# A median by bisection beside a convolution network: masks summed by TensorE in place of counting chunks on VectorE

## What is computed

```python
q_in = jnp.quantile(x.reshape(B, C, -1), 0.5, axis=-1)
x = x + jax.nn.relu(-q_in)[:, :, None, None]
y = upfirdn2d(x, lpf, up=2, padding=padding, gain=4.0)
y = jnp.maximum(y, 0.0)
y = upfirdn2d(y, lpf, down=2, padding=0, gain=1.0)
# second layer, shortened
spec = jnp.fft.rfft2(x, norm='ortho')
gate = sigmoid(w2 @ gelu(w1 @ abs(spec)))
xf = x + jnp.fft.irfft2(spec * gate, norm='ortho')
out = attention(q(xf), keys_and_values(xf)) @ proj_w + proj_b + x
```

## Time and profile before

| | |
|---|---|
| median of 3 runs | 12846.2 us (12845.59 to 12851.24) |
| the profiled execution | 12841.47 us, span 12840.0 us |
| PE busy | 10730.5 us (84%) |
| PEld busy | 5483.5 us (43%) |
| DVE busy | 9433.9 us (73%) |
| ACT busy | 7283.6 us (57%) |
| POOL busy | 2610.8 us (20%) |
| mean granted TensorE clock | 0.904 of 2.4 GHz |
| GpSimd's addition into Z (L1216) | 64 times, 4.5 us each |

### The profile page before, as it was taken

The page is one execution under the profiler, slowest core; times in us unless marked ns, Lnnn a source line. Parts: engine busy times, 40 slices in busy tenths (PEclk is TensorE's granted clock), DMA queues, the critical chain, the costliest instruction groups (busy, mean ns, idle before and its releaser), DMA issues. The chain is left out here.

```text
span 12840.0 us, 193091 instructions
## 1 busy us (share of the span) xinstructions
PE 10730.5 (84%) x70049; PEld 5483.5 (43%) x70049; DVE 9433.9 (73%) x16044; ACT 7283.6 (57%) x12109; POOL 2610.8 (20%) x4040
## 2 busy tenths in 40 slices
PE   1797888978879798897988889788897887979889
PEld 1543535334353443534435354353534435344353
DVE  7867667776777767768777686767777677776776
ACT  4656455564646646466464565646566464664646
POOL 1211202112131221302212021121211213122130
PEclk9898898988989899898998989889898898989989
DMA  1021120211202022120211202112021221202212
GB/s 45 18 43 42 39 61 18 50 35 43 57 26 55 21 49 52 28 67 7 54 47 34 66 13 46 43 40 60 18 53 31 45 56 27 53 21 49 52 28 66
DMA packets 169035, 532.27 MB, mean 41 GB/s; under 512 B 64008, under 2 KB 86536, under 8 KB 153168
## 3 DMA queue, kind: packets, MB, share of 16 engines
q1 hardware_dynamic: 168016, 519.00, 17.2%
HBM read 230.38 MB, written 67.11 MB: 23 GB/s over the span
## 5 line engine op out<-in xcount | busy, mean ns | idle before, releaser
L949 DVE TENSOR_REDUCE R<-ps 128x2 f32<-128x640 f32 x4096 | 3195.4, 818 | 941.5 <-PE ps L687 930.6
L1157 ACT ACTIVATE R<-ps 128x512 f32<-128x512 f32 x5120 | 2823.2, 594 | 671.5 <-PE ps L708 645.3
L236 ACT ACTIVATE R<-R,st 128x1475 bf16<-128x1475 f32 x1326 | 2022.9, 1526 | 862.5 <-DVE st L312 687.6
L300 DVE TENSOR_SCALAR_CACHE_REDUCE R<-R,st 128x1255 bf16<-128x1255 f32 x1326 | 2012.0, 1517 | 21.3
L687 PE MATMUL ps<-KST,R 96*128 96x320 bf16 x8192 | 1888.4, 314 | 60.7 <-DVE R L949 50.5
L733 PE MATMUL ps<-R 128*32 128x512 f32 x12288 | 1648.8, 609 | 38.0 <-DVE Wk L903 32.9
L708 PE MATMUL ps<-R,KST 104*128 104x512 bf16 x4096 | 1583.7, 389 | 21.4 <-ACT R L1157 20.6
L687 PEld LDWEIGHTS ps<-KST,R 96*128 96x128 bf16 x8192 | 764.8, 100 | 828.6 <-DVE R L949 313.0
L1245 POOL CAST R<-Wk 128x512 bf16<-128x512 f32 x256 | 283.8, 1109 | 2980.4 <-DVE Wk L903 2980.4
L201 PE MATMUL ps<-st,cst 128*128 128x3 f32 x884 | 176.0, 269 | 697.7 <-DVE R L300 464.4
L480 PE MATMUL ps<-R,cst 128*64 128x512 f32 x2048 | 648.5, 715 | 109.0 <-DVE R L818 109.0
(11 more groups left out here) (208 smaller groups left out, 19968.1 us busy)
## 6 DMA issues: line engine op xcount, KB each, us to landing
R<-R SPq DMA_DIRECT2D x3072, 64.0 KB, 2.4
R<-xh_in SPq DMA_DIRECT2D x136, 512.0 KB, 4.5
...
```

The source lines that it names most:

```text
L236: e.activation(junka[:, 0:o2 - o1], xc[:, o1:o2], ACT.Sign, bias=mid, scale=-1.0, accum_out=cnt[:, NP + i:NP + i + 1]).then_inc(md_ca, 1)
L300: e.tensor_scalar(junk[:, 0:o1 - o0], xc[:, o0:o1], mid, None, ALU.is_le, ALU.add, accum_out=cnt[:, i:i + 1]).then_inc(md_cv, 1)
L949: e.tensor_reduce(MX[(4 * u + s4) % 2][:, blk_, h0:h0 + 2], ps[:, 2 + 2 * bq:4 + 2 * bq, 0:320], axis=AX.X, op=ALU.max).then_inc(mx, 1)
L1157: e.activation(PB[:, t % 2, w, :], ps[:, w % 2, :], ACT.Exp).then_inc(ex, 1)
```

## The change

In each of the 26 steps VectorE writes two masks of 2560 columns (2.0 where the value is at most the midpoint, bf16), ScalarE takes signs of two chunks of 1536, TensorE adds the masks up over partition halves in 32 products of 160 columns with a 64-column weight `pairb`, into PSUM bank 7, and VectorE sums the 160 columns there. A step keeps three parts; the third holds the products and that sum. The bracket is plus and minus the largest magnitude: four reductions in four parts, the first midpoint 0, and all bracket widths by one product with a constant row `halves`. The recount is dropped; the masks of the minimum pass (now bf16, BIG a power of two) are added up by TensorE too. That pass goes to the parts right behind the search. ScalarE runs the first part of a pass ahead of the Relu instead of behind it. GpSimd adds the edge rows into Z four rows at a time, in four passes (for the last 16 rows all four in pass 36), and the transfers and the FFT groups wait for those counts. SyncE's last load of TAP2 waits for the end of the median. The mask buffers use the free end of R1. The diff, without the closing chain's renumbered waits; of the median's generators only the new lines and their surroundings are shown ("..." also stands where old lines went):

```diff
-NP = 3
-CUTS = [HALF * i // NP for i in range(NP + 1)]
-MIDS = [a + int(0.46 * (b - a)) for a, b in zip(CUTS, CUTS[1:])]
-SIGNED = sum(b - m for m, b in zip(MIDS, CUTS[1:]))
-FEWER = float(RANK - SIGNED)
+MASKS = ((0, 2560), (4096, 6656))
+SIGNS = ((2560, 4096), (6656, 8192))
+SUM = 160
+SIGNED = sum(b - a for a, b in SIGNS)
+FEWER = 2.0 * (RANK - SIGNED)
 P = C // 2
 MID = 5
...
@@ -85,9 +86,10 @@
...
-        junk = R5[:, 0:1024].bitcast(BF16)
-        junka = R5[:, 1024:2048].bitcast(BF16)
-        tmp = R5[:, :]
+        MK = [R5[:, 0:1280].bitcast(BF16), R1[:, 8320:9600].bitcast(BF16)]
+        junka = R5[:, 1280:2048].bitcast(BF16)
+        MF = [R5[:, 512 * i:512 * i + 512].bitcast(BF16) for i in range(2)]
+        TF = [R5[:, 1024:2048], R1[:, 8320:9344]]
...
@@ -186,29 +188,46 @@
                 self.reader = (md_g, self.asked)
 
         def pe_median(e, b7):
...
+            def sums(mask, width, first, last):
+                n = mask.shape[1] // (2 * width)
+                for q in range(n):
+                    for j in range(2):
+                        o = width * (2 * q + j)
+                        op = e.matmul(ps[64 * j:64 * j + 64, 7, 336:336 + width], lhsT=pairb[:, :], rhs=mask[:, o:o + width],
+                                      start=first and q == 0, stop=last and q == n - 1)
+                return op
+
+            for _ in range(4):
                 yield
             e.wait_ge(md_v, 1)
             b7.free(e)
...
+            e.matmul(P0(1), lhsT=c("swap"), rhs=pm[:, 0:1], start=True, stop=True).then_inc(md_p, 1)
             b7.ask()
             for k in range(STEPS):
...
+                yield
+                yield
+                e.wait_ge(md_cv, 2 * k + 2)
+                b7.free(e)
+                sums(MK[0], SUM, True, False)
+                sums(MK[1], SUM, False, True).then_inc(md_s, 1)
+                b7.reader = (md_r, k + 1)
+                yield
+                e.wait_ge(md_ca, 2 * k + 2)
+                b7.free(e)
+                e.matmul(P0(3), lhsT=c("pair"), rhs=cnt[:, 0:3], start=True, stop=True).then_inc(md_p, 1)
+                b7.ask()
+            for i in range(9):
+                if i < 8:
+                    e.wait_ge(md_ta, i + 1)
+                    b7.free(e)
+                    sums(MF[i % 2], 128, i == 0, i == 7).then_inc(md_fs, 1)
+                yield
+                if i > 0:
                     yield
...
+            b7.reader = (md_r, STEPS + 1)
             b7.free(e)
...
+            e.matmul(P0(1), lhsT=c("pair"), rhs=cnt[:, 0:1], start=True, stop=True).then_inc(md_p, 1)
             b7.ask()
...
             e.wait_ge(md_row, 1)
             b7.free(e)
             e.transpose(ps[0:1, 7, 384:512], pm[:, 0:1], c("ident")).then_inc(md_p, 1)
@@ -224,27 +243,27 @@
             e.matmul(ps[:, 7, 448:512], lhsT=ones[:, :], rhs=dg, start=True, stop=True).then_inc(md_p, 1)
 
         def act_median(e):
...
+            for _ in range(4):
                 yield
             for k in range(STEPS):
                 mid = mids[:, k % 2:k % 2 + 1]
                 e.wait_ge(md_v, 2 + k)
...
+                for i, (o1, o2) in enumerate(SIGNS):
                     if k or i:
...
+                        e.wait_ge(md_ca, 2 * k + i)
                     e.activation(junka[:, 0:o2 - o1], xc[:, o1:o2], ACT.Sign, bias=mid, scale=-1.0,
...
+                                 accum_out=cnt[:, 1 + i:2 + i]).then_inc(md_ca, 1)
                     yield
...
                 yield
+            for _ in range(17 + 2):
+                yield
 
         def pool_median(e):
...
+            for _ in range(4):
                 yield
             for k in range(STEPS):
                 mid = mids[:, k % 2:k % 2 + 1]
...
+                for i in range(3):
                     yield
                 e.wait_ge(md_g, 2 + k)
                 if k:
@@ -252,13 +271,12 @@
...
             for i in range(9):
                 if i < 8:
...
                     e.wait_ge(md_ta, i + 1)
...
+                    if i > 1:
+                        e.wait_ge(md_mm, i - 1)
+                    e.tensor_tensor(TF[i % 2], MF[i % 2], xc[:, 1024 * i:1024 * i + 1024], ALU.add).then_inc(md_tb, 1)
                 yield
                 if i > 0:
                     yield
@@ -269,73 +287,57 @@
             for k in range(4):
                 if halves[k // 2] is not None and k % 2 == 0:
                     e.wait_ge(halves[k // 2], 32)
...
+                e.tensor_reduce(m1[:, k:k + 1], xc[:, 2048 * k:2048 * k + 2048], axis=AX.X, op=ALU.max,
+                                apply_absolute_value=True).then_inc(md_got, 1)
+                yield
+            e.wait_ge(md_got, 4)
+            e.tensor_reduce(pm[:, 0:1], m1, axis=AX.X, op=ALU.max).then_inc(md_v, 1)
+            e.memset(mids[:, 0:1], 0.0)
             e.wait_ge(md_p, 1)
...
+            e.tensor_copy(other[:, 0:1], P0(1)).then_inc(md_g, 1)
             e.wait_ge(md_g, 1)
...
+            e.tensor_tensor(hi, other[:, 0:1], pm[:, 0:1], ALU.max).then_inc(md_got, 1)
+            e.wait_ge(md_got, 5)
+            e.tensor_scalar(hs, c("halves"), hi, None, ALU.mult).then_inc(md_v, 1)
             for k in range(STEPS):
                 mid, then = mids[:, k % 2:k % 2 + 1], mids[:, (k + 1) % 2:(k + 1) % 2 + 1]
                 e.wait_ge(md_v, 2 + k)
...
+                for i, (o0, o1) in enumerate(MASKS):
+                    e.tensor_scalar(MK[i], xc[:, o0:o1], mid, 2.0, ALU.is_le, ALU.mult).then_inc(md_cv, 1)
                     if i == 0 and k:
...
                         e.tensor_tensor(hi, hi, lift, ALU.min).then_inc(md_raise, 1)
                     yield
+                e.wait_ge(md_s, k + 1)
+                e.tensor_reduce(cnt[:, 0:1], ps[:, 7, 336:336 + SUM], axis=AX.X, op=ALU.add).then_inc(md_r, 1)
+                yield
                 e.wait_ge(md_p, 2 + k)
...
+                e.tensor_reduce(gg, P0(3), axis=AX.X, op=ALU.add).then_inc(md_g, 1)
                 if k < STEPS - 1:
                     e.wait_ge(md_g, 2 + k)
                     e.tensor_scalar(uu, gg, FEWER, hs[:, k + 1:k + 2], ALU.is_lt, ALU.mult).then_inc(md_got, 1)
...
+                    e.wait_ge(md_got, 6 + k)
                     e.scalar_tensor_tensor(then, uu, hs[:, k + 2:k + 3], mid, ALU.subtract, ALU.add).then_inc(md_v, 1)
...
             e.tensor_tensor(hi, hi, lift, ALU.min).then_inc(md_v, 1)
             e.wait_ge(md_v, STEPS + 2)
...
             for i in range(9):
                 if i < 8:
...
                     if i > 1:
...
+                        e.wait_ge(md_tb, i - 1)
+                        e.wait_ge(md_fs, i - 1)
+                    e.tensor_scalar(MF[i % 2], xc[:, 1024 * i:1024 * i + 1024], hi, BIG, ALU.is_le, ALU.mult).then_inc(md_ta, 1)
                 yield
                 if i > 0:
...
                     e.wait_ge(md_tb, i)
...
+                    e.tensor_reduce(mm[:, i - 1:i], TF[(i - 1) % 2], axis=AX.X, op=ALU.min).then_inc(md_mm, 1)
                     yield
+            e.wait_ge(md_fs, 8)
+            e.tensor_reduce(cnt[:, 0:1], ps[:, 7, 336:464], axis=AX.X, op=ALU.add).then_inc(md_r, 1)
             e.wait_ge(md_mm, 8)
...
+            e.wait_ge(md_p, STEPS + 2)
+            e.tensor_scalar(gg, P0(1), (RANK + 0.5) * BIG, None, ALU.is_ge).then_inc(md_g, 1)
...
@@ -507,7 +509,7 @@
                 if n < 16:
                     k = n % 2
                     e.wait_ge(zz, n + 1)
-                    e.wait_ge(zad, n // 4 + 1)
+                    e.wait_ge(zad, n + 1)
                     if n > 1:
                         e.wait_ge(s1, n - 1)
                     else:
@@ -1038,13 +1040,13 @@
                         e.wait_ge(yw_ps, n - 1)
                         e.wait_ge(tm, n - 1)
                     e.activation(T1[n % 2].rearrange("p h c n -> p h (c n)"), ps[:, 0:2, 0:266], ACT.Copy).then_inc(t1, 1)
+                slot(1 if n > 1 else 0)
                 m = n - 1
                 if 0 <= m < P:
                     e.wait_ge(yw_ps, m + 1)
                     if m > 1:
                         e.wait_ge(dn_ps, m - 1)
                     e.activation(Y[m % 2], ps[:, 2:4, :], ACT.Relu, scale=4.0).then_inc(yr, 1)
-                slot(1 if n > 1 else 0)
                 if n >= 8 and n % 8 == 0:
                     b = n // 8 - 1
                     e.wait_ge(mw_ps, b + 1)
@@ -1208,12 +1210,13 @@
                     e.wait_ge(rb, b + 1)
                     part = V[gq % 2][:, :, o:o + 2, 61:67]
                     e.tensor_tensor(part, part, RB[b % 2][:, :, 2 * (m % 8):2 * (m % 8) + 2, :], ALU.add).then_inc(vr, 1)
-                if n >= 12 and n % 8 == 4:
-                    b = n // 8 - 1
+                if n >= 12 and n % 8 > 3:
+                    b, i = n // 8 - 1, n % 8 - 4
                     e.wait_ge(zst[b], 96)
                     e.wait_ge(zz, 4 * b + 4)
-                    rows = Z[:, 16 * b:16 * b + 16, :]
```

(7 more changed lines are left out.)

90 lines of the change are left out of this document (12 added, 78 removed).

## The result

The changed kernel takes 13176.12 us (median of 4 runs, 13163.81 to 13183.63); the kernel before, on the same chip, 12847.34. The ratio is 1.0255, 95% interval 1.0237 to 1.0272. The profiled execution took 13171.03 us, its span is 13169.7, its mean granted clock 0.921. The forecast of 12776, faster, was wrong, and 13176 lies above its range.

What follows compares the result with a forecast made beforehand. VectorE was taken to lead the front (busy 182 of 210 us), in handshakes with TensorE and ScalarE. Terms: -3.8 us a body, -61 for sixteen, -9 first median; 12841.5 to 12771, plus 4.7, 12776; range 12560 to 13060.

Steps and rivals of the forecast that it cites:

- which I take as nothing: Search step in the front: 2.9 us less VectorE work against waits of 3.2 for 0.6 per two steps; -0.3, taken as nothing.
- In the other step the products hide under the copies: Every other search step: products hidden, but the count product has TensorE's next products in front of it, 1.2 us.
- The last count: Transposes: recounts (8 x 1.28) go, minimum pass moves in, +2.8 us a body; inverse -4.4; first median's recounts -11.7.
- The bracket: Four reductions for eight, -9.1 us a body; one product for 26 halvings, -4.0; more search parts in the front, +7.5.
- The quarters: Addition into Z in quarters of 1.13 us: of 9.5 us a body stood behind it, a quarter stays, -7.
- Waits behind GpSimd and behind masks: Front: 44 masks behind GpSimd at 0.1 us, +4 a body; minimum waiting 0.2 more in 22 steps, +4.4.
- the rival that doubled these terms: Waits behind GpSimd and bank 7 at twice their 13 us, less the clock's part: +6 a body, 12872, chance 0.15.
- Bank 7: PSUM bank held in two of three parts, later edge products, longer product chain at low clock: 0 to +10, taken +5.
- The slower rival: Search products cost more than their columns, 1.9 us a step instead of 1.3: +17 a body, 13064, chance 0.22.
- The clock rival: Products in TensorE's gaps may keep its clock at 2.4 GHz: -12.5 us a body, 12576, chance 0.18.
- The first median: Median standing alone: -9.1 - 4 - 11.7 for recounts + 26 x 0.6 for products at low clock, -9 us.
- the weight load's new wait: SP's last weight load waits for the median's end, early in the inverse: costs nothing.

Runs made afterwards that it cites:

- e3: The kernel before with only the bracket taken from the largest magnitude; 12609.65 us, 0.9812.
- e8: The kernel before with the bracket from the largest magnitude and the addition into Z in quarters; 12575.42 us, 0.9789.
- e12: The kernel with bracket and quarters (e8), plus ScalarE's search part ahead of its Relu copy; 12598.52 us, 0.9807.
- e11: The changed kernel with the last count as before: eight recounts, and the minimum pass without products; 12964.03 us, 1.009.
- e16: e15 without the products of the search's masks, so masks and signs alone, part of the count left out; 12335.94 us, 0.9593.
- e15: e11 with the search's 32 products made but their sum neither read nor waited for, part of the count left out; 12889.08 us, 1.0028.
- e1: The changed kernel with 4 products in a search step instead of 32, so counts cover part of the data; 12815.91 us, 0.9973.
- e13: The changed kernel with the minimum pass's products one part later in TensorE's order; 13041.63 us, 1.0151.
- e18: e11 with one mask and two counts a step, ScalarE's order of before, and the 16 products and read in the third part; 12629.55 us, 0.9823.

## Why the prediction was wrong

The five steps below lead from the kernel before (12853 in the first set; 12850 to 12853 in all sets) to the changed one (13176), 323 us, along kernels that differ in one part each (with the search step goes the wait ahead of SyncE's last load, which was not tried alone):

| from, to | what changes | measured | in my sum |
|---|---|---|---|
| before, e3 | bracket | -244 | about -103 |
| e3, e8 | addition into Z in quarters | -34 (-67 alone) | -112 |
| e8, e12 | ScalarE's order | +23 | 0 |
| e12, e11 | search step | +366 | about +182 |
| e11, after | last count from the masks | +212 | about -37 |

My column takes the per-body terms times 16 and the first median's share: bracket (-9.1 - 4.0 + 7.5) x 16 - 13; search (+4 + 4.4 + 5 - 3) x 16 + 15.6; last count (+2.8 - 4.4) x 16 - 11.7. The terms of the FFT stage and the inverse belong to several parts, so the column is a rough division.

- **The search step, "which I take as nothing", is the step that failed.** The prices in it were right (1.55, 0.32 and 1.30 us for 1.52, 0.32 and 1.3). The balance was not. I set 1.43 us of VectorE's work a step against VectorE's waits. From e12 to e16, where masks replace counts and no product is added, that work with its two signs for three gives 263 us. Putting the products back (e16 to e15) takes 553, reading their sum 75. 553 us over 17 medians of 26 steps are 1.25 us a step, and the front alone gives the same (27.3 us for 22 steps). That is the products and TensorE's stand ahead of them together, and that it comes near the 1.30 of the products is chance: by e1, 28 of the 32 products cost 0.81 us a step with the stand unchanged. In the terms of the prediction, VectorE's waits for sum and count were to be 3.2 us per two steps, for 0.6 before. Measured in the last fronts: 49.4 us in 22 steps, so 4.5 per two, for 12.0 in 20, so 1.2.
- **"In the other step the products hide under the copies"** was the reason given for charging half of them, and it is wrong. The sum's read waits 1.2 us or more in 17 of the 22 steps: in all 11 in which the second mask is the last part of a pass, as forecast, and in 6 of the other 11. Where nobody waits for the sum, the copies wait for TensorE's own down product instead: 24.7 us in e15's front. I asked who waits for the added result and not who waits for what now comes after it on TensorE. VectorE being the busiest engine (182 of 210) hid that front, copies and counts form one ring through both engines, in which most of an addition on TensorE shows.
- **TensorE's wait for the mask** was missing. In program order it reaches the products before the second mask is written and idles 24.4 us a front. The kernel before idled nearly as long for its counts (22.1), but the products that followed the wait were 0.5 us and not 1.3. e13 and e18 show what such a place costs: 135 and 79 us returned for the same instructions one part later.
- **The last count** was priced at the gate alone, and the removed recounts were taken as time won. Removing them brings the minimum pass forward into the FFT stage, where TensorE now stands at masks that it never waited for before (5.8 us there, 5.6 in the gate's stage). The size for transposes with gate (+1.3 for +2.8) was near only because the bracket's gain stands against it: without that, e11 to after, it is +4.9.
- **The bracket** was worth more. I charged 7.5 us a body for four more search parts in the front, -5.6 with the work that goes; the front grew by 2.4. And I gave the FFT stage nothing for losing four parts; it lost 9.6 us.
- **The quarters** gave a fraction of the 7 us. Alone 67 us, 4.2 a body; behind the bracket 34. The mechanism is as forecast, its size was not: 89 of the 152 us above the undisturbed durations stay, where I had put a quarter.
- **Waits behind GpSimd and behind masks** (+4 and +4.4): the waits are there, but smaller. The minimum (L309) waits 40.5 us over the whole run, 2.4 a median; a mask takes 1.62 us in the mean for 1.55 in the median, 3.6 a median. With the masks alone the kernel is faster than any other, so the rival that doubled these terms was wrong.
- **Bank 7** (+5, with the clock) is inside the step from e15 to e11, and so, with the sum's read and wait, at most 3.8 a body (788.9 to 792.7). TensorE's wait for the readers of bank 7 ahead of the products (3.6 and 1.8 us in the last front) is in the other step, e16 to e15. So the size of +5 was fair, but no run shows it by itself.
- **The slower rival** (13064) had its sign and nearly its size, but by a mechanism that is not there: the 32 products take 1.30 us, 81 ns a pair with everything in it. By the rate of the Trainium skill's page "TensorE: Matmul & The Clock Gate", LDWEIGHTS, two loads alone would be 107 ns a pair; the measurement decides against it for this pattern. **The clock rival** had its first half: the granted clock of the last front rose from 0.85 to 0.90, and from 0.86 in e16 to 0.92 in e15, so it moves with the products. Its second half failed: the shorter products of the front, 35.2 for 39.2 us at the down product from e16 to e15, did not make up for what was added.
- The first median came out as forecast (-8.8 for -9), partly by luck: the bracket gave -9.1 there for -13.1, the search step +12.9 for +15.6, the last count -12.4 for -11.7. No cost of the weight load's new wait shows: the convolution stage is unchanged, 50.0 and 50.2 us.
